# A recurrence followed by attention on one core: half of batch 0's front moved between the last 64 steps, and the masks of the diagonal score blocks written by ScalarE

## What is computed

```python
xn = layernorm(x)
# layer 0: a state recurrence over the 512 tokens, and a gated cell over the 8 batches
h = tanh(h @ A + u_t @ Bm);  y = h @ C.T + u_t @ D.T      # u = xn @ W_in + b_in
y = g_t * y + (1 - g_t) * xn_t                            # g = sigmoid(xn @ W_gate + b_gate)
s = y @ W_out + b_out + xn
c = sigmoid(..f) * c + sigmoid(..i) * tanh(..c)           # per step, xt @ w.T + c @ u.T + b
g = tanh(xn @ wo.T + c_final @ uo.T + bo)
x = x + s * silu(g);  xn = layernorm(x)
# layer 1: causal attention with 16 heads of 16 channels, and a mixture over 32 prototypes
s = softmax(where(causal, q @ k.T / 4, -inf)) @ v @ W_proj.T / 16
g = sum over the 2 nearest prototypes of weight * (A[i] @ (B[i] @ xn) + bias[i])
x = x + s * silu(g)
```

## Time and profile before

| | us |
|---|---|
| three runs, median | 1073.25 |
| lowest and highest | 1070.49, 1073.43 |
| the profiled execution | 1071.2 |
| its span on the core | 1069.4 |
| last cell state there, cell output starts | 359.88 |
| first score product of batch 0 | 413.49 |
| first unit of the first stage | 427.35 |
| first units of the four stages of a batch in the middle | 589.49, 610.82, 630.39, 648.36, and 670.12 for the next batch |
| busy TensorE, VectorE, ScalarE, GpSimd | 1008.3, 499.9, 515.8, 198.6 |

### The profile page before, as it was taken

The page is one execution under the profiler, slowest core; times in us unless marked ns, Lnnn a source line. Parts: engine busy times, 40 slices in busy tenths (PEclk is TensorE's granted clock), DMA queues, the critical chain, the costliest instruction groups (busy, mean ns, idle before and its releaser), DMA issues.

```text
span 1069.4 us, 20287 instructions
## 1 busy us (share of the span) xinstructions
PE 1008.3 (94%) x6526; PEld 684.7 (64%) x6526; DVE 499.9 (47%) x1147; ACT 515.8 (48%) x1384; POOL 198.6 (19%) x224
## 2 busy tenths in 40 slices
PE   6999999999999787899999999999999999999986
PEld 3677777777777653565665665665665666665653
DVE  5031123312121445565566566566566566566541
ACT  3344454444444422465465465465465465453433
POOL 5020111001000314204204204204204204200000
PEclk9999999999999987999999999999999999999999
DMA  8421112101003028052262263253253253225110
GB/s 250 150 71 67 59 49 69 40 31 59 29 29 128 20 99 177 22 173 55 71 190 56 70 186 60 69 185 61 69 182 64 69 178 68 70 85 104 32 40 20
DMA packets 66437, 93.75 MB, mean 88 GB/s; under 512 B 11872, under 2 KB 52832, under 8 KB 66400
## 3 DMA queue, kind: packets, MB, share of 16 engines
q1 hardware_dynamic: 60128, 88.83, 29.4%
q10 hardware_dynamic: 6272, 4.46, 1.3%
HBM read 59.41 MB, written 33.59 MB: 87 GB/s over the span
## 4 chain that ended last, share of the span: by engine, by line
PE 83%; DVE 6%; ACT 3%; issue 3%; DMA 1%; ACTq 1%; SPq 0%; POOL 0%; DVEq 0%; POOLq 0%
PE PS L843 26%; PE PS L1057 7%; PE PS L954 6%; PE PS L1006 6%; PE PS L1022 5%; PE PS L987 5%; PE PS L920 4%; PE PS L830 4%; PE PS L899 3%; PE PS L1088 3%; DVE nm L1740 3%; PE PS L941 2%; PE PS L1008 2%; PE PS L1044 2%; PE PS L1066 1%
## 5 line engine op out<-in xcount | busy, mean ns | idle before, releaser
L843 PE MATMUL PS<-arena 128*128 128x256 f32 x1024 | 313.7, 421 | 0.0
L1740 DVE TENSOR_REDUCE nm<-PS 128x1 f32<-128x512 f32 (+3 forms) x352 | 207.2, 636 | 89.9 <-PE PS L1008 89.8
L1390 ACT ACTIVATE arena<-PS 128x512 f32<-128x512 f32 x256 | 152.1, 600 | 169.8 <-PE PS L1044 169.7
L1251 ACT ACTIVATE arena<-PS 64x8 f32<-64x8 f32 x512 | 88.4, 173 | 184.9 <-PE PS L830 182.2
L830 PEld LDWEIGHTS PS<-arena 128*72 128x72 f32 x1024 | 128.8, 141 | 70.5 <-ACT arena L1251 7.3
L843 PEld LDWEIGHTS PS<-arena 128*128 128x128 f32 x1024 | 155.5, 192 | 0.0
L1022 PE MATMUL PS<-Q,K 98*128 98x512 bf16 (+3 forms) x512 | 120.4, 300 | 9.6 <-ACT arena L1390 5.1
L1590 DVE SCALAR_TENSOR_TENSOR arena<-arena 128x512 f32<-128x512 f32 x16 | 11.1, 694 | 249.1 <-ACT arena L1262 249.1
L830 PE MATMUL PS<-arena 128*72 128x8 f32 x1024 | 122.3, 192 | 0.0
L1006 PE MATMUL PS<-K,Q 96*128 96x256 bf16 (+3 forms) x512 | 112.9, 303 | 3.9 <-DMA K<-qk_d 1.8
L1008 PE MATMUL PS<-negmask,identb 128*128 128x128 bf16 (+2 forms) x352 | 86.8, 247 | 0.0
(11 more groups left out here) (189 smaller groups left out, 1293.1 us busy)
## 6 DMA issues: line engine op xcount, KB each, us to landing
qk_d<-QB SPq DMA_DIRECT2D x24, 512.0 KB, 3.0
Q<-qk_d SPq DMA_DIRECT2D x32, 192.0 KB, 3.9
K<-qk_d SPq DMA_DIRECT2D x32, 192.0 KB, 4.3
gt_d<-arena SPq DMA_DIRECT2D x16, 256.0 KB, 2.5
wx_d<-arena SPq DMA_DIRECT2D x16, 256.0 KB, 2.4
XT<-xt_d SPq DMA_DIRECT2D x8, 512.0 KB, 4.4
GT<-gt_d SPq DMA_DIRECT2D x8, 512.0 KB, 5.7
WX<-wx_d SPq DMA_DIRECT2D x8, 512.0 KB, 6.6
```

The source lines that it names most:

```text
L843: mm = pe.matmul(o, lhs, rhs, start=first, stop=last, skip_group_check=True)
L1390: s_.activation(PR[:, g % 2, j, at:at + T], PS[:, bank, :], ACT.Exp, scale=SCORE_SCALE).then_inc(t_e.sem, 1)
L1740: v_.tensor_reduce(nm[:, g, h:h + n, i], PS[:, u % 3, 0:n * (i + 1) * P].rearrange("p (n w) -> p n w", n=n), AX.X, ALU.max, negate=True).t ...
```

## The change

Two things are changed.

*The front.* The last iteration of the recurrence is written out instead of looped, and functions are called after given steps. TensorE: after steps 1, 2, 6 and 13 of its first half the prototype lengths, the cell output, the mix and the leave for tokens 0 to 255 of batch 0; after steps 5, 9 and 11 of its second half their transposes, their query product and their key product. ScalarE: two tanh after steps 8 and 10. VectorE has the w_qk copies, the gate opening and XNB between its cell updates of the iteration before, and the gating, residual, statistics, normalising and three-part split between those of the last one. GpSimd has the memset of VA in the fifth iteration and the deviations in the last one. SyncE loads batch 0's inputs after the fifth iteration. After the recurrence the same steps follow for tokens 256 to 511 alone, with VectorE where GpSimd or ScalarE had some of them. SyncE waits before the loads of head group 2 until the maxima of group 0 have arrived.

*The score blocks.* A unit is now one block of 128 keys x 128 queries for each of the four heads of the group, in the order of `UNITS`. The four diagonal units (0, 3, 6, 8) use bank 4, the six others bank 3. Others start their bank afresh; diagonal ones add to what is in the bank, which ScalarE wrote after the last diagonal exponential (`write_edge`), after the side work of that step. A unit waits for the exponential, or the write, of the last unit of its kind. The mask products are gone, but for one in the whole kernel (`edge_bank`).

```diff
+UNITS = ((0, 0), (0, 1), (0, 2), (1, 1), (0, 3), (1, 2), (2, 2), (1, 3), (3, 3), (2, 3))
+EDGES = tuple(n for n, (kt, q) in enumerate(UNITS) if kt == q)
@@ SyncE
             for g in range(G):
+                if g == 2:
+
+                    sp.wait_ge(m_ld[0].sem, m_ld[0].at(0, 2))
                 load_operands(0, g, False)
@@ GpSimd, last iteration
+            pool.wait_ge(c_u[1].sem, c_u[1].at(B - 1, 1))
+            pool.wait_ge(n_st.sem, n_st.at(0, NT))
+            g_.tensor_tensor(rst[:, 0:HT], mv[:, 0:HT, 1], eps[:, 0:HT], ALU.add).then_inc(f_rs, 1)
...
@@ TensorE, last iteration
+            half(B - 1, 0, 1, None, {1: prototype_lengths, 2: early_cell_out, 6: early_mix, 13: early_leave})
+            half(B - 1, 1, 1, None, {5: early_turn, 9: early_query, 11: early_key})
+
             pe.wait_ge(c_c.sem, 8 * B + c_c.credit)
             pe.wait_ge(c_t.sem, 16 * B + c_t.credit)
...
+            cell_out(0, range(HT, NT)).then_inc(f_pe, 1)
+            pe.wait_ge(q_r.sem, q_r.at(0, 2))
@@ TensorE, a unit
-                pe.wait_ge(t_e.sem, t_e.at(b, g * TQ + k - 1))
...
-                pe.matmul(edge, identb[:, :], negmask_t[:, :].unsqueeze(1).to_broadcast([P, n, P]),
-                          start=False, stop=True).then_inc(t_mm.sem, 1)
+                kt, q = UNITS[k]
+                edge = kt == q
+                before = [n - TQ * (n >= k) for n in range(TQ) if (UNITS[n][0] == UNITS[n][1]) == edge]
+                pe.wait_ge(t_e.sem, t_e.at(b, g * TQ + max(before) + 1))
+                for j in range(GH):
+                    h = g * GH + j
+                    mm = pe.matmul(PS[:, 3 + edge, j * P:(j + 1) * P], K6[0:KM, h, kt * P:(kt + 1) * P],
+                                   Q6[0:KM, h, q * P:(q + 1) * P], start=not edge, stop=True,
+                                   skip_group_check=True)
+                mm.then_inc(t_mm.sem, 1)
@@ TensorE, after recurrence
-            for m in range(KT):
-                mix(0, m, False)
-            pe.wait_ge(f_p2, 1)
+            half_mix(1)
             fill(FILL[0])
-            for n in range(2):
-                leave(0, n)
+            half_leave(7, 1)
             fill(FILL[1])
...
@@ ScalarE
+            half(B - 1, 0, 1, None, {8: early_hidden, 10: early_gate})
+            half(B - 1, 1, 1, None)
...
+            def write_edge(b, g, k):
+
+                act.wait_ge(t_x.sem, t_x.at(b, g * len(EDGES) + EDGES.index(k) + 1))
+                s_.copy(PS[:, 4, :].rearrange("p (j q) -> p j q", q=P),
+                        negmask_t[:, :].unsqueeze(1).to_broadcast([P, GH, P])).then_inc(t_e.sem, 1)
...
                 for k in range(TQ):
                     exp(b, g, k)
                     run(side, k)
+                    if k in EDGES:
+                        write_edge(b, g, k)
@@ VectorE, last iteration
+            gated_rows(5, 0)
+            half(B - 1, 0, 1)
+            dve.wait_ge(f_mr, 2)
...
+            half(B - 1, 1, 1)
```

More of the change, by code:

```diff
@@ L801, in late_project, with half @@
                 project_in(6, xtl[e], b_u.sem)
-            def half(b, n, late, it):
+            def half(b, n, late, it, side={}):
                 work = []
@@ L856, in _ @@
                           start=True, stop=True)
-            for late in range(2):
-                with pe.Fori(0, B // 2) as it:
-                    for n in range(2):
[L861 to L868, removed]
+            with pe.Fori(0, B // 2) as it:
+                for n in range(2):
+                    half(it, n, 0, it)
@@ new lines, in _, with prototype_lengths @@
+            with pe.Fori(B // 2, B - 1) as it:
+                for n in range(2):
+                    half(it, n, 1, it)
+            def prototype_lengths():
+                pe.wait_ge(init, 3)
+                pe.wait_ge(b_xt.sem, b_xt.at(B // 2, 0))
+                pe.wait_ge(b_ue.sem, b_ue.at(B // 2, 0))
+                for k in range(KT):
+                    mm = pe.matmul(PS[:, 6, 0:NP], ones[:, :], ptsq[:, k], start=(k == 0), stop=(k == KT - 1))
+                mm.then_inc(f_pp, 1)
@@ new lines, in cell_out, with early_cell_out @@
+            def cell_out(bank, of):
+                for j in of:
+                    for k in range(KT):
+                        mm = pe.matmul(PS[:, bank, j % 2 * D:(j % 2 + 1) * D], CT[:, k, j * P:(j + 1) * P],
+                                       w_uo[:, k], start=(k == 0), stop=(k == KT - 1))
+                return mm
+            def early_cell_out():
+                pe.wait_ge(ld_b, 16 * len(loads_b))
+                pe.wait_ge(c_c.sem, c_c.at(B // 2, 0))
+                cell_out(5, range(HT)).then_inc(f_u, 1)
@@ new lines, in half_leave, with early_leave @@
+            def half_leave(bank, n):
+                pe.wait_ge(y_p.sem, y_p.at(0, n + 1))
+                for j in (2 * n, 2 * n + 1):
+                    for k in range(KT):
+                        mm = pe.matmul(PS[:, bank, j % 2 * D:(j % 2 + 1) * D], YS[:, k, j * P:(j + 1) * P],
+                                       w_out[:, k], start=(k == 0), stop=(k == KT - 1))
+                mm.then_inc(s_mm.sem, 1)
+            def early_leave():
+                pe.wait_ge(f_e, 1)
+                half_leave(5, 0)
@@ L1017, in maxima_turn, with edge_bank @@
                              ).then_inc(m_t.sem, 1)
[L1019 to L1023, removed]
+            def edge_bank():
+                pe.wait_ge(c_w.sem, c_w.at(B, 0))
+                pe.matmul(PS[:, 4, :].rearrange("p (n w) -> p n w", n=GH), identb[:, :],
+                          negmask_t[:, :].unsqueeze(1).to_broadcast([P, GH, P]), start=True, stop=True)
             def turned(b, g, k):
```

334 lines of the change are left out of this document (226 added, 108 removed).

## The result

The change makes the kernel slower. Its median is 1093.06 us (1089.35 to 1094.8), that of the kernel before, measured beside it, 1072.51 (1070.49 to 1073.43); the ratio is 1.019, with a 95% interval of 1.016 to 1.022. The forecast was 1058.5. The profiled execution took 1092.63 us for a span of 1090.7, at a mean granted clock of 0.952; the kernel before had 0.984.

What follows compares the result with a forecast made beforehand. Bounds: latency in batch 0's front, a two-engine loop in the recurrence, TensorE in attention. Front -14.3, mask product +0.2, seven cycles -1, first stage -0.3, last batch +0.7: -14.7, so 1058.5 us; 8 in 10 from 1040 to 1070.

Steps and rivals of the forecast that it cites:

- The front: Batch 0's start: half moved into the recurrence costs 8.6 us, the shorter chain behind it gains 22.9, net -14.3.
- Rival D: Recurrence: an insert's wait comes late and moves later steps, about 10 us given back, 1069 to 1073; chance 0.08.
- A unit costs 0.22 us: Score blocks on TensorE: four 128-column products take 0.22 us, ten units 2.2 instead of 3.1 a stage.
- rival B: Score blocks: weight loads pace the 128-column products, 1.7 us more a batch, +14 or 1072 us; chance 0.05.
- The mask write takes 0.59 us: ScalarE's 128x512 write into PSUM takes 0.59 us, after the exponential and side work; edge units wait for it.
- The wait at the end of the fourth stage: Next batch's first unit waits for weight copies (0.9) and the write (0.5), 0.6 saved upstream: +0.8, net +0.45 us.
- the end of the third stage: Stage four's first unit needs write 8 and comes 0.4 us later; TensorE stands about 1.3 us.
- The last batch: No side work: stages -0.5, 0, -0.8, then +2.0 in the units-only last stage; together +0.7 us.
- clock 1.00 from the first stage on: Attention: TensorE keeps its full clock, since it stayed there through all waits of the earlier profile; no cost counted.
- Rival A: Stage boundaries don't hold; most of the 0.89 us a stage arrives: 1031 in full, 1045 at half; chance 0.17.
- Rival C: Mask writes hold TensorE at every edge unit, ScalarE sets the pace; one us a stage gives 1089; chance 0.12.
- The saving turned into waits: Attention: TensorE's 0.89 us a stage is real but becomes waits at two of four boundaries; seven cycles about -1.

Runs made afterwards that it cites:

- e1: The changed kernel's front alone, with score blocks as in the kernel before: 1060.25 us, ratio 0.990 to the kernel before.
- e4: The changed kernel plus filler products on TensorE ahead of stages and distances, eight a batch, results unread: 1069.0 us, ratio 0.998 to the kernel before.
- e5: The changed kernel with diagonal blocks as units 0, 2, 4 and 6, writes still behind side work: 1069.76 us, ratio 1.000 to the kernel before.
- e7: The changed kernel with only unit 8's mask write moved ahead of that unit's side work: 1072.63 us, ratio 1.002 to the kernel before.
- e3: The changed kernel with all ScalarE mask writes directly behind their exponentials, ahead of side work: 1077.26 us, ratio 1.006 to the kernel before.
- e12: The changed kernel with masks by TensorE instead of ScalarE, and unit 8's fourth-stage exponential computed three times: 1087.63 us, ratio 1.016 to the kernel before.
- e2: The changed kernel's score blocks alone, with the front of the kernel before: 1100.6 us, ratio 1.0285 to the kernel before.

## Why the prediction was wrong, point by point

- **The front** (-14.3): right in mechanism and nearly in size. Recurrence end forecast "near 368.5", measured 366.88; "first scores near 399", measured 399.88; first unit 14.1 earlier by the sum, 12.8 measured, -10.7 us on the whole kernel in e1, inside the bounds -19 to -9. That it came so near is in part luck: the inserts cost 7.0 us instead of 8.6, and the chain behind the recurrence takes 33.0 instead of 30.7. Rival D is out: the inserts met no late wait, the first score product came before 405.
- **A unit costs 0.22 us** (rival B): right. In the change eight products in a row, two units, stand as follows:

```profile
623.05 0.61 PE L1126 MATMUL PS<-Q,K 98*128 98x128 bf16 x8
```

  One unit alone shows 0.39 to 0.40, so the second adds 0.22, or 0.055 a product. The page "TensorE: Matmul & The Clock Gate" of the Trainium skill, section "Back-to-back issue gap", gives 81 ns for such a stream; this trace, which has up to eight in a row, does not agree, and B is out.
- **The mask write takes 0.59 us** and the next unit waits for it behind the side work: right (128 writes, mean 591 ns). The second stage is 0.35 us shorter in the trace (19.22 against 19.57), as forecast with 0.3.
- **The wait at the end of the fourth stage** was mis-sized: forecast +0.8 us over the 0.70 of rows 6, measured +1.3 to +1.7. At the end of the third stage I had about 1.3, measured 1.00. The last batch was mis-sized too: forecast +0.7, measured +6.4 with what follows it, and still +5.3 against e1 in the profiled execution of e4, where its clock is low in places.
- **The step that failed** is the clock: "clock 1.00 from the first stage on, since it stayed there through all waits of rows 1". That sentence was false, and the trace of before could have told me. In its last batch TensorE waits 1.62 us for a transfer, and this follows (order of events, then the busy time of that stretch):

```profile
1024.20 0.39 PE L1022 MATMUL PS<-Q,K 98*128 98x512 bf16 x1 [1.62 <-DMA Q<-nml]
...
1025.40 4.01 PE L1057 MATMUL PS<-arena 128*32 128x512 f32 x32
```

```profile
1024.20:1030.00 5.80, 5.80 (x46) 2.24 (x47) 1.89 (x3) 0.70 (x2) 0.00 (x0) 0.71 0.00 0
```

  The same products by V take 2.36 at 1053.77. Over 632.65 us such a stretch is rounded away to 1.00; I read the mean and not the places behind the longest waits, then forecast waits of 1.3 us and more with no price for the clock. A price stood there: 4.01 - 2.36 = 1.65 us for one set, and over two starts in each of seven batches, 23 us. e4 puts this term at 24 us. But the agreement is partly luck. The two long waits that I forecast were those ahead of the fourth and the first stage; behind the one ahead of the fourth (1.00 us) the clock held, and the second place where it fell, the third stage, has only 0.54 us ahead of it, where I had forecast no loss at all. Apart from the clock the forecast would still have been short, by 9 us against e1: forecast -0.1 us a batch, measured +1.0 with fillers (e4) and +0.3 where the waits are spread and the clock holds (e5).
- **Rival A** is out, with a batch of 85.25 where it needed 78. **Rival C** had the right sign and size (1089), but for another reason, so its size is luck. It took ScalarE for the pace of the whole stage. e5 has all of ScalarE's added load and runs at 80.9 a batch where the clock holds: the load eats TensorE's saving, it does not make the kernel slow. "One over 82.5 makes C right" was the wrong test, as a low clock gives the same number; clock and batch length have to be read together.
- **The saving turned into waits**, as I had said of two boundaries, by its whole amount: in a batch e5's TensorE is busy 2.4 us less and idle 2.7 more.

## What to carry to other kernels

Work taken off TensorE is worth nothing if its next instruction waits for an in-order queue that has got longer, and a wait that grows from 0.7 to 2 us can cost twice: once for itself and once more for the products behind it at half clock. Before forecasting a clock, read it not as a mean over the stages but behind the longest waits that the trace has, and give each wait that grows in the changed kernel that price as a term of its own. This finds only a part of such places: at the third stages here a wait that grew from 0.32 to 0.54 us was enough. Where a wait cannot be removed, a few idle products in it show at once how much of the loss is the clock; where a release stands behind side work in an engine's queue, move that one release first (e7).

## What was not expected of the hardware

- The clock fell to 1.2 GHz behind waits of 1.1 to 2.4 us, and at the third stages behind waits of 0.4 to 0.8 us followed by the distance products, and stayed low through dense work: from 668.93 TensorE has no gap for 6 us, and the products by V from 671.07 still take 4.08 us instead of 2.36.
- Equal waits in one execution (1.53 and 1.52 us in e3, 1.87 in e12) had it fall in some batches and not in others.
- In e2 the loss repeats itself once it has set in: the products by V of a first stage take 2.4 us at 509.1, 4.0 at 591.6, and 4.0 to 4.3 in all later batches. In e3 and e12 it comes and goes.
- ScalarE wrote a broadcast bf16 mask of 128x512 into PSUM in 591 ns, as long as its copies out of PSUM (587).
